# Three of 392 gather units of a graph-and-expert kernel fetched row by row by SyncE instead of GpSimd

## What is computed

```python
# x (6250, 256) f32, src, dst (100000,) int32; src is sorted along with dst, so its values are in no order
def _L0_gnn_ref(x, W1, b1, W2, b2, edge_index):
    dst = edge_index[0]; nbr = edge_index[1]          # here: edge_index = [src, dst]
    agg = segment_sum(x[nbr], dst, n)                 # gather 100000 rows of 1 KB, sum them by node
    cnt = segment_sum(ones, dst, n)
    mean = agg / maximum(cnt, 1)
    return x @ W1.T + b1 + mean @ W2.T + b2
def _L0_ffn_ref(x, ...):                              # 8 experts, the best 2 of each row, 256 -> 1024 -> 256
    ...
x = x + _L0_gnn_ref(_layernorm(x), ...)
x = x + _L0_ffn_ref(_layernorm(x)[None], ...)[0]
```

## Time and profile before

| | us |
|---|---|
| median of 3 runs | 1964.03 (1962.31 to 2257.03) |
| the profiled execution: its time / the span on the core | 1958.99 / 1956.9 |
| granted TensorE clock, mean | 0.976 |
| busy: PE / POOL / ACT / DVE | 1768.8 / 1193.3 / 1117.8 / 967.5 |
| edge stage, first to last gather issued by POOL | 108.3 to 1147.4 |
| expert stage, about | 1161 to 1957 |

### The profile page before, as it was taken

One profiled execution on the slowest core, in us unless ns is written; L12 is line 12 of the kernel. 1 busy time (PEld: TensorE's weight loads), 2 busy tenths in 40 slices (PEclk: granted clock), 3 DMA queues, 4 the chain that ended last, 5 costly groups with the idle time before them and its releaser, 6 DMA issues.

```text
span 1956.9 us, 41490 instructions
## 1 busy us (share of the span) xinstructions
PE 1768.8 (90%) x11167; PEld 1495.9 (76%) x11167; DVE 967.5 (49%) x2315; ACT 1117.8 (57%) x3316; POOL 1193.3 (61%) x1141
## 2 busy tenths in 40 slices
PE   6888998899887898878877879999999999999997
PEld 4655875588555677656665768999999999999997
DVE  6868977898467787633334786311111111111111
ACT  5964875477544699755652657544444444444443
POOL 1167777788777777777777743444554454544543
PEclk9989999999999899999999989999999999999999
DMA  9333333333333333344443767724424424242421
GB/s 313 101 88 103 95 98 102 101 90 86 100 104 103 100 97 95 104 127 139 144 138 110 243 229 236 222 36 128 125 40 121 98 66 120 39 127 38 124 36 20
DMA packets 113112, 224.31 MB, mean 115 GB/s; under 512 B 27286, under 2 KB 76604, under 8 KB 107094
## 3 DMA queue, kind: packets, MB, share of 16 engines
q0 software_dynamic: 61152, 129.45, 26.7%
q1 hardware_dynamic: 32576, 74.98, 11.2%
q10 hardware_dynamic: 19254, 18.32, 3.0%
HBM read 371.77 MB, written 34.91 MB: 208 GB/s over the span
## 4 chain that ended last, share of the span: by engine, by line
PE 46%; POOL 31%; issue 11%; DMA 6%; DVE 4%; SPq 1%; ACT 1%; DVEq 0%; POOLq 0%; ACTq 0%
POOL arena L650 31%; PE bank L1315 19%; PE bank L1331 18%; DMA arena<-ytab,arena 4%; PE bank L1280 2%; PE bank L1055 2%; PE bank L1101 1%; PE bank L1303 1%; DMA gw<-in_gw2t 1%; SPq L465 1%; DVE agg L1949 1%; DMA ytab<-arena 1%; DMA agg<-in_b 0%; DMA agg<-xtab_a,arena 0%; PE bank L1255 0%
## 5 line engine op out<-in xcount | busy, mean ns | idle before, releaser
L650 POOL DMA_INDIRECT arena<-ytab,arena x784 | 800.6, 1021 | 240.1 <-issue 230.9
L1280 PE MATMUL bank<-arena 128*128 x2356 | 631.4, 395 | 111.4 <-SPq L525 109.9
L1280 PEld LDWEIGHTS bank<-arena 128*128 128x128 f32 x2356 | 415.2, 197 | 212.8 <-issue 151.7
L948 ACT ACTIVATE arena<-bank,agg 128x128 f32<-128x128 f32 x840 | 308.4, 367 | 403.7 <-PE bank L1315 345.7
L1315 PEld LDWEIGHTS bank<-arena,agg 128*128 128x128 f32 x3360 | 392.2, 193 | 5.8 <-issue 1.0
L1315 PE MATMUL bank<-arena,agg 128*128 128x128 f32 x3360 | 393.8, 276 | 0.6 <-issue 0.6
L1949 DVE TENSOR_TENSOR agg<-agg,bank 128x257 f32 x589 | 248.1, 421 | 294.1 <-PE bank L1280 254.6
L1331 PE MATMUL bank<-agg,arena 128*128 128x256 f32 x1680 | 380.1, 380 | 0.4 <-DMA agg<-in_b 0.4
L683 POOL DMA_INDIRECT out<-arena x105 | 170.8, 1627 | 324.2 <-issue 241.4
L1331 PEld LDWEIGHTS bank<-agg,arena 128*128 128x128 f32 x1680 | 311.5, 190 | 38.2 <-DMA agg<-in_b 0.7
L794 ACT ACTIVATE arena<-lanes,arena 128x128 f16<-128x128 f16 x816 | 247.9, 386 | 19.3 <-DVEq L1577 19.3
(11 more groups left out here) (275 smaller groups left out, 1661.5 us busy)
## 6 DMA issues: line engine op xcount, KB each, us to landing
agg<-in_w SPq DMA_DIRECT2D x210, 1024.0 KB
agg<-in_b SPq DMA_DIRECT2D x105, 128.0 KB
arena<-ytab,arena POOLq DMA_INDIRECT x784
ytab<-arena SPq DMA_DIRECT2D x12, 512.0 KB, 3.2
arena<-in_xt ACTq DMA_DIRECT2D x24, 256.0 KB, 3.0
node<-in_x SPq DMA_DIRECT2D x6, 896.0 KB, 12.3
agg<-in_xt SPq DMA_DIRECT2D x6, 896.0 KB, 12.9
out<-node ACTq DMA_DIRECT2D x6, 896.0 KB
```

The source lines that it names most:

```text
L650: pool.indirect_dma_start(out=rows[:, v % RU, h, 0:D], out_offset=None, in_=ytab[:, :], in_offset=bass.IndirectOffsetOnAxis(ap=rowidx[g % ...
L948: act.activation(hT[:, m, :], hidden_bank(j, m)[:, 0:T], ACT.Relu, bias=b1b[:, b, m:m + 1]).then_inc(s_fr, 1)
L1280: mm = pe.matmul(bank[bank_of(n)][:, 0:W], onehot[n // QUAD % 2][:, n % QUAD, h, :], pair[:, h * W:(h + 1) * W], start=(h == 0), stop=(h = ...
```

## The change

- Three units, number 80 of group 1, 112 of group 2 and 118 of group 3 (units 143, 261 and 385 of all), are left out of POOL's loop. POOL issues 6 of its 784 gathers less.
- SP fetches their 768 rows one at a time: each is a DMA of its own with a register as row number, from `ytab` to one partition of one of two new buffers behind the eight (`BUFFERS = 2`). The 256 rows of a unit are spread evenly over the SP iterations of that group: over 78 iterations in group 1 (3 or 4 each), 110 in group 2 (2 or 3) and 116 in group 3 (2 or 3). Before every 16th row SP loads 16 row numbers from the new table `row_list`. In the group's first iteration it also waits for `s_ones` and for `s_tab`.
- The row numbers of the single unit come into one partition by two small multiplications on PE for each group, and a copy on DVE. `rows_listed` has one more short operation ahead of `s_lane` and `s_rowtab`, and `segment_units` two more to point `slot` at the new buffer.
- The arena grows from 23100 to 25200 floats for each partition, and `dynamic_dma_scratch_size` is set to 8192 bytes (its default is 16384).

```diff
+ALONE = [(), (80,), (112,), (118,)]
+ROWS_EACH = HALVES * P
+ALONE_UNITS = [UNIT0[g] + k for g in range(NG) for k in ALONE[g]]
+BUFFERS = 2
...
+def gathered_into(v):
+    return sum(1 for u in range(v % RU, v + 1, RU) if u not in ALONE_UNITS)
...
-        ROOM = 23100
+        ROOM = 25200
...
-        rows_flat = take(RU * HALVES * W)
+        rows_flat = take((RU + BUFFERS) * HALVES * W)
         rows = rows_flat.rearrange("p (r h w) -> p r h w", h=HALVES, w=W)
+        row_list = [take(ROWS_EACH, I32) for _ in range(2)]
+        row_col = take(HALVES)
...
+            def single_rows(g, i, which):
+                n = alone_before(g) + i
+                for a in which:
+                    if a % 16 == 0:
+                        listed[:] = loaded(ENG.SP, row_list[g % 2], i * ROWS_EACH + a, 16, NP - 1)
+                    sp.dma_start(rows[a % P:a % P + 1, RU + n % BUFFERS, a // P, 0:D], ytab[bass.ds(listed[a % 16], 1), :]).then_inc(s_alone[n], 16)
+            def single_rows_beside(v):
+                g = max(g for g in G if UNIT0[g] <= v)
+                k = v - UNIT0[g]
+                if k == 0 and ALONE[g]:
+                    sp.wait_ge(s_ones, 1)
+                    sp.wait_ge(s_tab, g + 1)
+                    sp.sem_inc(s_pass)
+                for i, k_i in enumerate(ALONE[g]):
+                    single_rows(g, i, share((ALONE[g][i - 1] if i else 0, k_i - 2), ROWS_EACH, k))
...
             for v in range(UNIT0[NG]):
-                sp.wait_ge(s_row[v % RU], 16 * HALVES * (v // RU + 1))
+                if v in ALONE_UNITS:
+                    sp.wait_ge(s_alone[ALONE_UNITS.index(v)], 16 * ROWS_EACH)
+                else:
+                    sp.wait_ge(s_row[v % RU], 16 * HALVES * gathered_into(v))
                 sp.sem_inc(s_units)
                 if v >= BACK:
                     free(v - BACK)
+                single_rows_beside(v)
...
                     v = UNIT0[g] + k
+                    if v in ALONE_UNITS:
+                        continue
                     if v >= RU:
                         pool.wait_ge(s_free, v - RU + 1)
...
+                for c in range(HALVES * len(ALONE[s])):
+                    mm = pe.matmul(placed[0:1, c * P:(c + 1) * P], row_col[:, c:c + 1], ident[:, :], start=True, stop=True, skip_group_check=True)
                 mm.then_inc(s_e6, 1)
...
                 step(v.tensor_scalar(slot_t[0:1, 0:n], unit_i[0:1, 0:n], RU - 1, None, ALU.bitwise_and))
+                for i, k in enumerate(ALONE[s]):
+                    apart = RU + (alone_before(s) + i) % BUFFERS - (UNIT0[s] + k) % RU
+                    step(v.tensor_scalar(apart_t[0:1, 0:n], unit_i[0:1, 0:n], float(UNIT0[s] + k), float(apart), ALU.is_equal, ALU.mult))
+                    step(v.tensor_tensor(slot_t[0:1, 0:n], slot_t[0:1, 0:n], apart_t[0:1, 0:n], ALU.add))
...
+                for i, k in enumerate(ALONE[s]):
+                    begun(v.tensor_scalar(row_col[:, HALVES * i:HALVES * (i + 1)], w[1][:, HALVES * k:HALVES * (k + 1)], 0.0, None, ALU.max))
+                settle()
                 v.sem_inc(s_lane)
...
-    nc = bacc.Bacc("TRN2", target_bir_lowering=False, num_devices=1)
+    nc = bacc.Bacc("TRN2", target_bir_lowering=False, num_devices=1, dynamic_dma_scratch_size=8192)
```

More of the change, by code:

```diff
@@ L46, with alone_before @@
 ALL = SEG0[NG - 1] + RUN[NG - 1]
+ALONE = [(), (80,), (112,), (118,)]
+ROWS_EACH = HALVES * P
+ALONE_UNITS = [UNIT0[g] + k for g in range(NG) for k in ALONE[g]]
+BUFFERS = 2
+def alone_before(g):
+    return sum(len(a) for a in ALONE[:g])
+def gathered_into(v):
+    return sum(1 for u in range(v % RU, v + 1, RU) if u not in ALONE_UNITS)
 CHMAX, UMAX, SMAX = max(CH), max(UNITS), max(SEGS)
@@ L321, in gnn_moe @@
         lane_of = arena[:, room[0]:room[0] + HALVES * SMAX].rearrange("p (k h) -> p k h", h=HALVES)
-        unit_i, slot_t = take(SMAX, I32), take(SMAX, I32)
+        unit_i, slot_t, apart_t = (take(SMAX, I32) for _ in range(3))
         lane1 = take(CHMAX)
@@ L417, in gnn_moe @@
         s_row = [sem(f"rows_in{r}") for r in range(RU)]
+        s_alone = [sem(f"single_rows_in{n}") for n in range(len(ALONE_UNITS))]
         s_units, s_free, s_apart, s_oh16, s_oh, s_ohd, s_agg, s_sum = (sem(n) for n in ("units_in", "units_free", "lanes_apart", "onehot16_ready", "onehot_widened", "onehot_direct", "segment_multiplied", "segment_summed"))
@@ L520, in free @@
                 sp.sem_inc(s_free)
+            def single_rows(g, i, which):
[13 more added lines that the diff above has]
+                    single_rows(g, i, share((ALONE[g][i - 1] if i else 0, k_i - 2), ROWS_EACH, k))
             done = []
+            listed = []
             for v in range(UNIT0[NG]):
-                sp.wait_ge(s_row[v % RU], 16 * HALVES * (v // RU + 1))
+                if v in ALONE_UNITS:
+                    sp.wait_ge(s_alone[ALONE_UNITS.index(v)], 16 * ROWS_EACH)
+                else:
+                    sp.wait_ge(s_row[v % RU], 16 * HALVES * gathered_into(v))
                 sp.sem_inc(s_units)
@@ L1264, in _ @@
                         m = min(16, SEGS[g] - k)
-                        at = loaded(ENG.PE, slot[g % 2], k, m, (RU - 1) * HALVES * W)
+                        at = loaded(ENG.PE, slot[g % 2], k, m, (RU + BUFFERS - 1) * HALVES * W)
                         upto = [n_units & COUNTS for n_units in loaded(ENG.PE, need[g % 2], k // 2, m // 2, UNIT0[NG])]
@@ L1549, in lanes_kept @@
                 v.wait_ge(s_e6, s + 1)
+                m = ROWS_EACH * len(ALONE[s])
+                if m:
+                    begun(v.tensor_copy(row_list[s % 2][0:1, 0:m], placed[0:1, 0:m]))
                 v.tensor_copy(laneT[0:UNITS[s]].rearrange("p h q -> p (h q)"), misc[0:UNITS[s], 0:HALVES * P]).then_inc(s_laneT, 1)
```

## The result

| | before | after |
|---|---|---|
| median, us (lowest to highest) | 1963.17 (1961.13 to 2257.03) | 2031.43 (2028.81 to 2032.22) |
| ratio to before | 1 | 1.036 [1.0346, 1.0374] |
| span of the profiled execution, us | 1956.9 | 2029.9 |
| granted TensorE clock, mean | 0.976 | 0.945 |
| first / last gather issued by POOL, us | 108.3 / 1146.1 | 109.0 / 1218.9 |

The change made the kernel slower by 68 us, where the forecast was 1959.0 us and the range ended at 1986. One execution of before, the 2257.03 us, is a slow one and counts in no ratio. The loss arises in the edge stage: the last gather comes 73 us later, and from the last gather to the end it takes 811 us in both (1146.1 to 1956.9, now 1218.9 to 2029.9).

What follows compares the result with a forecast made beforehand. POOL's gather instruction time was taken to set the edge stage until 1106.64 us. Two units at 2.5 us save 5.0, added work costs nothing: 1964.0 - 5.0 = 1959.0 us, range 1954 to 1986.

Steps and rivals of the forecast that it cites:

- The step that failed: Arena behind the new buffers: moving by 1542 floats, an even number, was claimed to leave the old tables' load prices unchanged.
- The list loads are dear: Rival, SP's loads of 16 row numbers: 3.28 us each instead of 0.98, giving 1964 to 1969 us; chance 0.10.
- SP is overrun: Rival, SP's queue in the edge stage: dear row DMAs hold POOL up, 2004 or 2064 us; over 2% slower, chance 0.11.
- My 0.57: Forecast price in us of one row DMA on SP's queue, with address and gaps; 162 of 188 us in group 1.
- The static rows of 0.64 and 0.78: Static 1 KB row copies behind a 512 KB store, times in us; set aside as queue delay, 0.78 kept as upper bound.
- What is removed: POOL's gathers in the edge stage: 2.5 us a unit, two units counting, the third nothing; 5.0 us gained.
- The slack at the start of a group: POOL's wait for row numbers: 11.4 us of slack in group 2 and 13.8 in group 3 cover the gain.
- `s_tab`: SP's new wait at a group's first unit: tables of group 3 done at 827.6 us, costed at no wait.
- the added operations: Short operations in `rows_listed` and `segment_units` and a copy: covered, otherwise under 0.3 us each for a group for the latter.
- the PE products: Two small matrix products on PE for each group: priced at a few tenths of a us.
- The scratch: Scratch of 8192 bytes: costed at nothing; rival that gathers wait, 2003 us and more from 20 waits, chance 0.02.
- What would show it wrong: Sign in group 1: POOL waits for SP's release and SP for no landing; then check rows, addresses, list loads.

Runs made afterwards that it cites:

- e1: Kernel before with 2 empty floats behind the row buffers, so all behind them lies 8 bytes on; 2032.34 us, ratio 1.0361.
- e3: Kernel before with only the register tables and what lies behind them 8 bytes on; 2033.96 us, ratio 1.0373.
- e4: Kernel before with everything up to the register tables 8 bytes on and the tables 16 bytes on; 1960.42 us, ratio 1.0000.
- e2: Changed kernel with 2 floats left empty behind `row_col`, putting the tables back on the 16-byte boundary; 1952.35 us, 0.9955 of the kernel before.
- e9: Changed kernel with tables back on the boundary and group 3's single unit at 100 instead of 118; 1950.85 us, 0.9952 of the kernel before.
- e6: Kernel before with only DVE's table `offs` 8 bytes on, on a slower chip; 2117.91 us, ratio 1.0038.

## Why the prediction was wrong, point by point

**The step that failed** is this one: "The whole arena behind them moves by 1542 floats, an even number, so the old tables keep their parity and price." I had seen the effect, 0.98 against 3.28 us on one line of code, and had rightly put it down to where the table starts. From two starting points (0 and 4 bytes over) I made the rule "even float", without a case that told 8 bytes from 16. In its place e1, e3 and e4 show a multiple of 16 bytes: 8 bytes on, with nothing else changed, cost 71 us, and 16 bytes on cost nothing. And I asked only about the new list's own loads. The loads of PE and DVE, on the same kind of table and with 76 and 38 instances in the trace, stood in no term of the sum, though a wrong rule would move them all at once: that gives some 150 us of PE's queue by the prices above, and 40 us or more with PE's 110 us of waiting taken off, a loss that I could have worked out and named as a rival. Such a rival would still have missed the fall of the clock, with most of the 40.3 us of PE busy.

**"The list loads are dear"** was the rival next to it, priced at 1964 to 1969, and it looked at the wrong loads. The lists start on multiples of 16 bytes, their loads took 0.98 to 1.25 us for the most part, and the 16 us a unit forecast for them were 19.

The Trainium skill (Runtime: NRT & Kernel Launch, Instruction fetch mechanics), cited there, has register loads at about 200 ns each. The runs agree for tables off the boundary (DVE 3.61 / 16 = 0.226 us, SP 3.27 / 16 = 0.204) and not for those on it (1.10 / 16 = 0.069, 0.97 / 16 = 0.061). The Trainium skill (SBUF — State Buffer, Operand start alignment) says that an operand need only start at a multiple of its element size. The runs agree that such a table works; what it costs is what they add.

**SP is overrun** was wrong as a mechanism. POOL's waits for SP's release look like it, but a row costs 0.43 us and not the 0.87 that it needed. My 0.57 was itself 0.14 too high: the DMA takes 0.225 us and not the 0.34 of line 555, and what lies between two has no more than a FUSED_REGOPS of 0.037 and a MOVE of 0.029 us. The demand in group 1 was 129 us of 188 and not 162. The static rows of 0.64 and 0.78 were, as argued, no price for this.

**What is removed** was right in kind. In e2 POOL never waits, and of its 9 us the scratch has about 3, which leaves 6 against the 5.0 forecast; three such units before the chain leaves POOL gave 6.3 us (3 to 10). Neither is measured finely enough to confirm 2.5 us a unit. POOL issues 6 x 1.33 = 8 us less; 5 ns more for each of the other gathers took half of it back in the profiled execution. Unit 385 gave nothing by itself, as forecast. The chain of e2 leaves POOL for good at 1107.30 and not, as I had written, at 1101.6: the piece of the chain named below is the landing of its last gather there (start and length in us). Before it was 1106.64. The place where the chain leaves POOL did not come earlier although the stage's end did, so it was a poor mark of the gain:

```profile
1107.30 6.74 DMA arena<-ytab,arena
```

**The slack at the start of a group, `s_tab`, the added operations, the PE products** cost nothing that the traces of e2 or e9 show: one true wait of 1.6 us at L1600, as in the earlier trace rows.

**The scratch** was costed at nothing because no gather waits. None does, and yet it shortened the DRAIN at the program's end by 4.8 us, of which about 3 came through: the program ends with POOL's DRAIN, and I had not asked what its 8.69 us consist of. With both terms the sum for e2 would be 1958.99 - 5.0 - 4.8 = 1949.2 for the profiled execution, and its span of 1947.9 with 2.1 us around it is 1950.0. Part of that fit is luck: it is the fastest of the five executions of e2, whose median is 1952.35.

**"What would show it wrong"** listed POOL waiting for SP's release, and it does. It then told the reader to look at rows, addresses and lists. SP's waits at `free` for PE (377.9 us, from 25.6 in the rows shown of before) were the line that led out of this.

## What to carry over

When an edit changes the size of a buffer in a hand-cut arena, the addresses of everything behind it are part of the edit: list what moves, by how many bytes, and who reads it. Start each table that is loaded into registers on a multiple of 16 bytes. A price seen at two addresses gives no rule; take the coarsest alignment that fits both as the safe one, and price the other outcome over all instructions of that kind. And where an engine "issues" for 3.5 us in front of a matrix product, look at what its own queue loads, before believing the engine that the waits further down name.

## What the runs showed of the hardware

- A 16-value register load from an SBUF table mostly takes 0.97 (SP) or 1.10 us (PE, DVE) if the table starts on a multiple of 16 bytes from the arena's start, and 3.27 (SP; 4, 8 or 12 bytes over), 3.6 (DVE; 8 over) or 3.8 us (PE; 8 over) if it does not. The 8-value kind on PE goes from 0.59 to 1.93. The tiles between the row buffers and the tables (one-hot matrices, lanes, the row numbers of the gathers) moved by 8 bytes cost nothing (e4: 1.0000).
- PE stands still while its queue loads: in after, the 38 pauses that hold a pair of loads end 0.06 us after the second load, and the profile calls most of them "issue".
- A DMA of one 1 KB row with a register as its row number takes SP's queue 0.225 us, and 0.43 from start to start.
- POOL's DRAIN at the end of the program took 8.69 us with a scratch of 16384 bytes, 3.91 with 8192 and 3.74 with 4096.
- The mean of POOL's indirect gather (128 rows of 1 KB) varied between 1012 (e6) and 1032 ns (e9) over kernels and chips, which is 16 us on 780 gathers and more than a change of a few units is worth.
